# Two of eight LayerNorm groups per unit moved from ScalarE to GpSimd in the last phase of a metaformer kernel

## The reference

```python
# --- layer 1 ---
x = x + _L1_conv_ref(_ln_c(x), ...)      # ends in a 1x1 convolution and y * x
t = _to_tokens(x)
t = t + _L1_ffn_ref(_ln_t(t), W1, b1, W2, b2)
x = _from_tokens(t, x)

def _ln_t(v, eps=1e-5):                  # per token, over its 96 channels
    m = jnp.mean(v, axis=-1, keepdims=True)
    s = jnp.var(v, axis=-1, keepdims=True)
    return (v - m) / jnp.sqrt(s + eps)
```

## Time and profile before

| | us |
|---|---|
| runs, median of 3 | 3661.55 (3657.33 to 3664.26) |
| profiled execution | 3659.49 |
| its span, first to last instruction | 3657.6 |

### The profile page before, as it was taken

How to read it: one execution, slowest core, us unless ns; L and a number is a source line. 1 busy time by engine, 2 the same in 40 slices (tenths; PEclk the granted TensorE clock), 3 DMA queues, 4 the chain that set the end, 5 groups by cost and what they waited for, 6 DMA issues and landing times. The chain is left out here.

```text
span 3657.6 us, 68122 instructions
## 1 busy us (share of the span) xinstructions
PE 3017.4 (82%) x21990; PEld 1910.0 (52%) x21990; DVE 3218.4 (88%) x8131; ACT 2781.3 (76%) x6274; POOL 1728.9 (47%) x2404
## 2 busy tenths in 40 slices
PE   6787888878787878887876799997888888888887
PEld 5565665656565656565654344443444444444444
DVE  4888889898989898989886699999899999999998
ACT  2577777777777877777778455554799999999998
POOL 3777777777787877787864000000222222222221
PEclk9999999899999999999987899999999999999999
DMA  3233323232323232323212888897676667666762
GB/s 68 53 89 74 91 71 88 71 88 70 88 71 88 71 88 71 88 71 88 71 56 69 212 238 234 236 280 212 172 199 188 181 185 200 184 184 193 199 177 83
DMA packets 696178, 478.92 MB, mean 131 GB/s; under 512 B 407217, under 2 KB 674422, under 8 KB 683830
## 3 DMA queue, kind: packets, MB, share of 16 engines
q1 hardware_dynamic: 695830, 474.58, 49.2%
HBM read 272.09 MB, written 201.92 MB: 130 GB/s over the span
## 5 line engine op out<-in xcount | busy, mean ns | idle before, releaser
L1891 POOL TENSOR_SCALAR C_var<-C_st 128x16 f32<-128x16 f32 x64 | 13.5, 211 | 1338.6 <-DVE C_st L178 1338.6
L1464 DVE SCALAR_TENSOR_TENSOR B_y<-B_mid,B_coefs,B_y 128x512 f32<-128x512 f32 x768 | 509.0, 750 | 3.2 <-ACT B_y L1429 3.2
L1395 PE MATMUL B_ps_row<-B_z,B_band 128*128 128x512 f32 x1152 | 499.1, 596 | 15.1 <-DMA B_band<-edge_scratch 15.1
L378 DVE TENSOR_SCALAR A_hq<-A_h,A_b 128x512 f16<-128x512 f16 x768 | 319.4, 456 | 176.5 <-ACT A_h L370 169.6
L370 ACT ACTIVATE A_h<-A_hid 128x512 f16<-128x512 f32 x768 | 428.3, 594 | 59.5 <-PE A_hid L357 57.1
L178 DVE BATCH_NORM_STATS2 A_st<-A_xT 128x6 f32<-128x192 f32 x1536 | 443.6, 349 | 29.3 <-ACT A_xT L861 16.0
L370 ACT ACTIVATE C_h<-C_hid 128x512 f16<-128x512 f32 x768 | 425.0, 589 | 22.9 <-PE C_hid L357 22.5
L1504 ACT ACTIVATE C_q<-C_xT,C_shift,C_rstd 128x96 fp8e5<-128x96 f32 x1024 | 392.6, 457 | 43.3 <-POOL C_shift L1898 43.2
L894 ACT ACTIVATE A_xc<-A_xT,A_shift,A_rstd 128x96 f32<-128x96 f32 x1024 | 379.3, 456 | 4.2 <-POOL A_shift L1207 4.0
L167 POOL TENSOR_TENSOR A_rstd<-A_var,A_expo 128x16 f32<-128x16 f32 x128 | 376.5, 2941 | 10.7
L1395 PEld LDWEIGHTS B_ps_row<-B_z,B_band 128*128 128x128 f32 x1152 | 218.8, 190 | 294.2 <-issue 287.8
(11 more groups left out here) (167 smaller groups left out, 7248.7 us busy)
## 6 DMA issues: line engine op xcount, KB each, us to landing
A_xq<-in_x SPq DMA_DIRECT2D x32, 1536.0 KB, 8.9
x_scratch<-A_xT SPq DMA_DIRECT2D x64, 768.0 KB, 3.2
x_scratch<-A_x3h SPq DMA_DIRECT2D x64, 768.0 KB, 5.4
B_z<-x_scratch SPq DMA_DIRECT2D x96, 512.0 KB
y_scratch<-B_y SPq DMA_DIRECT2D x96, 512.0 KB, 3.6
C_x3q<-x_scratch SPq DMA_DIRECT2D x32, 1536.0 KB, 9.1
C_xT<-x_scratch SPq DMA_DIRECT2D x64, 768.0 KB, 16.6
C_y3q<-y_scratch SPq DMA_DIRECT2D x31, 1536.0 KB, 15.6
```

The costliest lines, as they stand in the source:

```text
L378: r = dve.tensor_scalar(self.hq[:, b, s], self.h16[:, b, s], self.w["b1"][:, j:j + 1], 0.0, ALU.add, ALU.max)
L1395: m = pe.matmul(bank(c, h), band[c.buf(NB)][:, d, :], z[c.buf(NB)][:, half(h), d:d + W], start=(d == 0), stop=(d == 2))
L1464: dve.scalar_tensor_tensor(y, mid[c.buf(2)][:, half(h), t:t + W], coefs[:, c.n, 3 + t:4 + t], y, ALU.mult, ALU.add).then_inc(ev["sums"], 1)
```

## The change

Group 3 of each half (groups 3 and 7 of a unit) leaves ACT. POOL computes it right behind the terms of the half, in two passes over 128 x 384: scaled = x * rstd in f32 into a new buffer, then q8 = scaled + shift as fp8. Slots 0 and 4 of ACT lose their `act_norm`; the slots of the six other groups stay. The events split: `norm2` now counts six ACT groups of a unit, `normp` two POOL groups, and every waiter asks `normed(i, k)` for the right one. `norm_terms` gets one wait more, since the terms of the unit before now have two readers, ACT's group 2 or 6 and POOL's group 3 or 7.

```diff
-LN_AT = {6: (1, 0), 7: (1, 1), 8: (1, 2), 0: (0, 3), 1: (0, 4), 2: (0, 5), 3: (0, 6), 4: (0, 7)}
+LN_AT = {6: (1, 0), 7: (1, 1), 8: (1, 2), 1: (0, 4), 2: (0, 5), 3: (0, 6)}
+POOL_GROUP = 3
@@ class RowFeedForward
+        self.scaled = sb("scaled", [P, TPC, C], F32)
+    def normed(self, i, k):
+        if k % 4 == POOL_GROUP:
+            return self.ev["normp"], self.ev.at("normp", i, k // 4)
+        return self.ev["norm2"], self.ev.at("norm2", i, k - k // 4)
+    def pool_norm(self, pool, i, k):
+        ev, t = self.ev, slice(k * TPC, (k + 1) * TPC)
+        pool.wait_ge(ev["ln2"], ev.at("ln2", i, k // 4))
+        earlier = i if k // 4 else i - 1
+        if begun(earlier):
+            pool.wait_ge(ev["normp"], ev.at("normp", earlier, 1 - k // 4))
+        if begun(i - 1):
+            pool.wait_ge(ev["q8_full"], ev.at("q8_full", i - 1, k))
+        x = self.x_of(i)[:, k * CW:(k + 1) * CW].rearrange("p (t c) -> p t c", c=C)
+        pool.tensor_tensor(self.scaled[:], x, per_token(self.rstd[:, t], TPC), ALU.mult).then_inc(ev["scaled"], 1)
+        pool.wait_ge(ev["scaled"], ev.at("scaled", i, k // 4))
+        pool.tensor_tensor(self.q8[:, t, :], self.scaled[:], per_token(self.shift[:, t], TPC), ALU.add,
+                           saturate=False).then_inc(ev["normp"], 1)
@@ pe_q8
-        pe.wait_ge(ev["norm2"], ev.at("norm2", i, k))
+        pe.wait_ge(*self.normed(i, k))
@@ norm_terms (POOL)
                 pool.sem_inc(ev.passed, 1)
                 if begun(q - 1):
-                    pool.wait_ge(ev["norm2"], ev.at("norm2", q - 1, 4 * half + 3))
+                    pool.wait_ge(*ff.normed(q - 1, 4 * half + 2))
                     pool.sem_inc(ev.passed, 1)
+                    pool.wait_ge(*ff.normed(q - 1, 4 * half + 3))
@@ body (POOL)
                         norm_terms(q, half)
+                        ff.pool_norm(pool, q, 4 * half + POOL_GROUP)
```

More of the change, by code:

```diff
@@ L1632, in phase_c @@
                 back_uses += [("y", s - 1, 0, "y16", s - 1), ("c", s - 1, 0, "out", s - 1)]
-        ev = Events(nc, ctx, "C_", dict(x1=NK, bn2=NK, ln2=2, ln2_s=6, norm2=NK, q8_full=NK, y_full=NK, c_full=NK, q8c=NK,
+        ev = Events(nc, ctx, "C_", dict(x1=NK, bn2=NK, ln2=2, ln2_s=6, norm2=NK - 2, normp=2, scaled=2, q8_full=NK, y_full=NK, c_full=NK, q8c=NK,
                                         hidden=NJ * NK, h16=NJ * NK, relu=NK, hq=NK, y16=NK, yb=NK, out=NK, pw_full=NK,
```

## The result

| | us |
|---|---|
| before, median of 4 | 3662.24 (3657.33 to 3664.26) |
| after, median of 4 | 3724.93 (3718.79 to 3728.30) |
| ratio after to before | 1.0171 (95% interval 1.0153 to 1.0190) |
| profiled execution after, and its span | 3728.04, 3726.0 |

What follows compares the result with a forecast made beforehand. Bound: the POOL-to-ACT chain in slot 1, ACT until slot 5, DVE from slot 6. Steps of +0.49 us gave +15.2, less 1.0 for step 31; 3659.49 + 14.2 = 3673.7, plus 2.1 for the median: 3676, range 3655 to 3696.

Steps and rivals of the forecast that it cites:

- the bound of slot 1: Slot 1: statistics, POOL terms, ACT norm of group 4, then C_y release DVE 7.0 us after the statistics.
- the triple of slot 5: DVE's three hidden passes in slot 5 shrink from 1.00 to 0.87 us, a gain of 0.13 a step.
- -1.0: Step 31, without a front part and paced by ACT until about slot 5, gains 1.0 us from losing slot 4's norm.
- So one meeting of 0.57 us: Slot 6: one first-half POOL pass holds DVE up once, costing the step 0.57 us; bounds 0 and 1.14.
- the second starts 0.9 to 1.1 us later, when L382 has begun: Slot 6: POOL's second first-half pass must wait for the running L382, then meets only DVE's PSUM readers, which slow nowhere.
- the step's sum: Per step: -0.13 for slot 5, +0.05 for one more wait, +0.57 for a held-up DVE pass, giving +0.49 us.
- the chain: Slot 1: statistics, POOL terms, ACT norm of group 4, C_y; 7.0 us, not shortened by the change.
- the added wait: One more, already satisfied wait in POOL's `norm_terms`, between 0 and 0.11 us, taken as 0.05 once a step.
- earlier against the statistics than 7.0 us: Sign of being wrong: in slot 1, C_y comes sooner than 7.0 us after DVE's statistics.
- the first rival: Both first-half passes meet a DVE pass, or one there and one in the second half: 1.06 a step, 3693; chance 0.17.
- Gain 0: Removing ACT's slot 0 norm gains nothing: C_y comes when it did, and DVE's slot 1 waits move before it.
- the rivals: Both first-half passes meet DVE, 3693 (0.17); no meeting, 3658 (0.14); relief reaches DVE, 3642 or 3624 (0.15); full-length holds, 3710 (0.05).

Runs made afterwards that it cites:

- first half placed: Changed kernel, POOL's two passes on group 3 made to wait for DVE's own events (ends of L382 and L1578 in slot 6): 3678.35 us, 1.0052.
- PE filled: Changed kernel plus idle matmuls on PE in both its stalls, 7 in slot 2's queue and 8 in slot 7's: 3692.97 us, 1.0091.
- relief alone: Changed kernel without POOL's passes; ACT still loses groups 3 and 7, whose normalised tokens stay zero: 3680.36 us, 1.0057.
- the best version: Changed kernel, all four POOL passes waiting for DVE's events, ACT's groups 4 to 6 normalised in slots 2 to 4: 3609.89 us, 0.9862.
- late terms on ACT alone: Kernel before, POOL unchanged, ACT normalising groups 4 to 7 one slot later, in slots 2 to 5: 3667.39 us, 1.0015.
- placed and filled: Changed kernel, first-half POOL passes waiting for DVE's events, plus 7 idle matmuls in PE's slot 1 stall: 3653.06 us, 0.9983.
- passes alone: Kernel before, ACT keeping all eight groups, POOL also running its passes into a spare tile nobody reads: 3707.35 us, 1.0136.

## Why the prediction was wrong

Right: the bound of slot 1. The norm taken from slot 0 bought DVE next to nothing, its wait came back in front of L1578 (1.56; forecast 1.5), the triple of slot 5 shrank to 0.87, and the second half's passes lay under that wait. Step 31 gained 1.1 us (from the last second-half shift to the end of the span it is 27.9 us instead of 29.0), where -1.0 was put. Right too that a POOL pass and DVE's L378 exclude each other, and that POOL work beside PSUM readers and statistics is free (first half placed). The Trainium skill, "SBUF — State Buffer", "Who interferes with whom", says of the shared port pair that tensor_scalar can take it in its 2-port modes, that whichever of the two engines issues first has it for the whole instruction while the other blocks, and that a DVE instruction with at most one SBUF input, outside those modes, does not contend with GpSimd. This case's runs agree where it concerns the passes: L378 and L382 are held up, and the held L378 ends only behind its pass, by 0.14 us; the gate, x4, the statistics and the output (first half placed) are not held up. What a meeting costs is still less than the 0.83 us of the pass: 0.65, as L378 by itself would have taken 0.35. What does not fit is POOL's power, some 3 us long: it holds no L378 up (371 ns at most before).

Wrong, first, the term "So one meeting of 0.57 us". Both passes met an L378, at 0.65 us each, 1.29 in all. The price was read as 0.57 in phase A; the number of meetings is the larger part of the miss. The step that failed is "the second starts 0.9 to 1.1 us later, when L382 has begun". I set the first pass 0.1 to 0.4 us behind shift, and the gap was 0.08; so it caught the second L378, not the third or L382. The second pass did come 0.91 later, as forecast; but DVE, held up by the first, still had its third L378 ahead. With 1.29 the step's sum is -0.13 + 0.05 + 1.29 = 1.21; 1.07 was measured. Most of the difference is the chain: the added wait is not the +0.05 of the sum (POOL starts the terms 0.41 us behind the statistics instead of 0.39), and with the shorter power L1578 comes 0.14 earlier behind them. By the sign that I had set ("earlier against the statistics than 7.0 us") the chain was wrong by that much. With -0.14 the sum is 1.02. Two meetings were the first rival, 1.06 a step and 3693, and with the clock held up, PE filled, the chip gives 3692.97. That its step fits within 0.01 is in part luck: its price, 0.57 for 0.65, is too low by about what its chain is too long.

Wrong, second, a term that was not in the sum, put at nothing without a reason: TensorE's clock. "Gain 0" for slot 0 asked only what DVE gains. The relief drew two waits of PE, 1.14 and 0.66 us, into one of 1.86, and the meetings in slot 6 made one of 1.96 out of 0.66. Behind either the granted clock halves for a while. The relief with its stall costs 21 us net (relief alone), both together 32 of the 62.7 (PE filled). None of the rivals had it, though the earlier trace rows show the clock at 1.00 as something that could be lost.

How the 62.7 us divide: 33.6 for DVE's hold-up less the gains (PE filled, 3692.97, less its own run of the kernel before, 3659.38), and 32.0 for the clock (3724.93 - 3692.97). The sum, 65.6, is over by 2.9, as each has another run of the kernel before. Open: why the clock falls in 22 of 31 steps and not in each, and how the best version's gain divides between placing and late terms. Placing the second half without late terms was not run, nor late terms without placing; placing the first half and filling gave 33.34, late terms on ACT alone 33.70, and all four passes placed with late terms 32.05. By slots, the best version gains on placed and filled in slot 1 (4.01 for 5.66) and slot 2 (3.83 for 3.96), and loses in slots 4 (4.16 for 3.94) and 5 (4.16 for 3.83); slot 6 is the same. So what it has over that kernel, it has at the place of the chain.

## What to carry to other kernels

Before moving work to GpSimd, lay its passes over VectorE's timeline: beside f16 tensor_scalar passes each costs VectorE most of its length (here 0.65 of 0.83 us), beside PSUM readers or statistics nothing, and a wait on VectorE's own event puts them there. Relieving the busiest engine pays only if the wait that ends last stands behind it; here it stood behind a POOL chain that an ACT queue passed on to DVE. And whenever waits are moved or merged, look at what PE does meanwhile: two short stalls may be harmless where one long one lowers the clock for the matmuls behind it.

## What the runs showed of the hardware

- Work taken off an engine and given to nobody made the kernel slower by 0.57% (0.42 to 0.72%), by way of the clock: stalls of PE of 1.86 us in each step come with a stretch of half clock in 30 of 31 steps (34.23 us on average), and the one step without lasts 33.35. In the kernel before, with stalls of 1.14 and 0.66 us there, the clock stayed 1.00 from 2700 to 3600 us.
- From 2700 to 3550 us the clock is 1.00 in each of the five kernels whose steps have no stall of PE over 1.14 us (placed and filled has a single one of 1.56), and falls in each of the five whose steps have one of 1.86 to 2.88 us.
- Fifteen matmuls a step that nobody reads made the kernel 32 us faster; seven made another one 25 us faster (first half placed against placed and filled).
- A POOL pass of 128 x 384 that an L378 waits for takes 0.83 us, as alone; the L378 takes up to 987 ns instead of 345 and ends some 0.14 us behind the pass. Behind an L382 that is still running it is POOL that waits: in passes alone 29 of the 64 second passes take over 0.9 us, up to 1.02.
